# First MLP of a fused cross-attention and mixture-of-experts kernel: both first-layer products in three parts of high and low numbers, one bias added a stage earlier, VectorE's work per block in another order

## The chip, the cores and the metric

The kernel runs on one core of a Trainium2 chip. The metric is the device time of one execution in microseconds (us); for the kernel before, the median of three runs is shown beside the lowest and the highest.

## The reference

The input is x, 64 x 64 tokens of 128 numbers, a context of 64 x 64 x 96 and the weights. Four layers are added to x in turn, each of the normalised x:

```
x = x + xattn0(layernorm(x), ctx)   # attention with the 32 largest scores, a convolution along time, an MLP
x = x + ffn0(layernorm(x))          # router, 8 experts, two a token, limited capacity
x = x + xattn1(layernorm(x), ctx)
x = x + ffn1(layernorm(x))          # 8 experts with low-rank parts
```

The part that the change touches is the end of xattn0 and the router of ffn0:

```
xt = x_text + y                                     # y: the convolution
h  = layernorm(xt, g_ffn, b_ffn)
h  = gelu(h @ W1 + b1) @ W2 + b2                    # 128 -> 512 -> 128
xt = xt + h
xattn0 = layernorm(xt, g_norm_out, b_norm_out)      # g_norm_out: "gout", b_norm_out: "bout"
...
x  = x + xattn0
n  = layernorm(x)
logits = relu(n @ rw1 + rb1) @ rw2 + rb2            # 128 -> 512 -> 8, two largest of 8
```

## The kernel before

The 4096 tokens are 32 tiles of 128 rows, and all of x lies in SBUF (`G.X`, and `G.XT` for the branch). The program is a row of stages, each a block with one program an engine, written by hand with semaphores: set-up, first attention, `convolution` (L1005 on), `first_mlp_and_router` (L1088 on), first experts, combination with the second attention, second experts, combination. The order of each engine's instructions is the order in which they are written; no scheduler changes it.

`first_mlp_and_router` works in 8 blocks of 4 tiles, 512 tokens each. Each engine has a loop over steps t, in which several blocks are at different points:

- VectorE (`block_statistics`, L189; `normalise_block`, L208): statistics of XT for the MLP's norm (block t+2, first root), normalised rows `mlp_xs`; the addition of the second product to XT (block t-1, L1374) and its statistics (second root); the output norm into `mlp_nb`, times gout (L1386), added to x (L1387), and statistics of x (third root); the normalised x of block t-2 into XT (`xn`), which the router reads and SyncE writes out.
- GpSimd computes the inverse roots (L203, L205), one after each statistics, and adds two biases a block (`add_biases`): b2 to XT (L1217) and bout to X (L1218). From the third call on it waits until VectorE has normalised `mlp_nb` (semaphore `gained`), as the biases stand behind the second root in its order.
- TensorE transposes the normalised rows (L1240), makes the hidden product, four fp32 matmuls of 128x512 (L1247, two instructions each in the trace), the second product (L1276, 16 of 128x128), and for the router: transposes (L1269), the first product (L1292, again four of 128x512), the logits in four column groups (L1262), and their sums over the groups (L1285).
- ScalarE takes the transposes out of PSUM (L1317 with the norm's gain and bias, L1339 for the router), the gelu (L1323), the relu (L1342) and the logits (L1335).

One step of TensorE, in order: transposes of block t+1, hidden product of t, logits of t-3, router transposes of t-2, second product of t, sums of t-3, first router product of t-2. Behind the loop VectorE picks the two largest logits: a batch of the first 28 tiles (from L1062 in the trace), then one of the last four.

The convolution stage runs 8 steps of 16 channels. TensorE's small products (L1035) feed VectorE's scaling (L1045) and shift (L1051), GpSimd adds the result to XT (L1025), and SyncE loads the MLP's weights (semaphore `weights`, 8 loads).

The second experts of the program already multiply in three parts: a number is split into a high part, rounded to the type F32R by ScalarE (L2417), and a low part, the rest (VectorE, L2446); L2403 to L2405 are high x high, low x high and high x low.

Of the kernel before, what the change touches and what calls it, by code (L numbers as in the profile page):

```python
# [6 lines left out]
F32 = mybir.dt.float32  # L7
# [8 lines left out]
P = 128  # L16
# [3 lines left out]
TB = 4  # L20
# [972 lines left out]
def convolution(nc, C, A, G):  # L993
# [4 lines left out]
    with ExitStack() as ctx:  # L998
# [4 lines left out]
        with nc.Block() as block:  # L1003
# [36 lines left out]
            def _(dve):  # L1040
                for g in range(NG + 1):
# [5 lines left out]
                    if g > 0:  # L1047
# [4 lines left out]
                                          ALU.add).then_inc(s["y_shift"], 1)  # L1052

# [34 lines left out]
def first_mlp_and_router(nc, C, A, G):  # L1088
# [9 lines left out]
    with ExitStack() as ctx:  # L1098
        def two(name, shape):
            return [C.sb(f"{name}{j}", shape, ctx=ctx) for j in range(2)]  # L1100

        w1, rw1, w2, rw2, b2, gout, bout, rb2 = (G.mlp[n] for n in ("w1", "rw1", "w2", "rw2", "b2", "gout", "bout", "rb2"))
# [31 lines left out]
            "xs", "turned", "xf", "y", "y_taken", "biased", "gained", "xn", "turned1", "xf1", "logits", "logits_sb", "summed", "lg", "pick",  # L1134
# [28 lines left out]
        with nc.Block() as block:  # L1163
# [27 lines left out]
            def _(pool):  # L1191
# [22 lines left out]
                def add_biases(b):  # L1214
                    rows = slice(b * TB, (b + 1) * TB)
                    pool.wait_ge(s["xs"], b + 1)
                    pool.tensor_tensor(G.XT[:, rows, :], G.XT[:, rows, :], wide(b2[:].unsqueeze(1), [P, TB, D]), ALU.add)  # L1217
                    pool.tensor_tensor(G.X[:, rows, :], G.X[:, rows, :], wide(bout[:].unsqueeze(1), [P, TB, D]), ALU.add).then_inc(s["biased"], 1)  # L1218

                for t in range(-2, NBLK + 1):  # L1220
# [5 lines left out]
                    root_of(1, t - 1)  # L1226
                    if blk(t + 1):
                        if blk(t - 1):
                            pool.wait_ge(s["gained"], t)
                        add_biases(t + 1)  # L1230
# [3 lines left out]
            def _(pe):  # L1234
# [7 lines left out]

                def hidden(b):
                    pe.wait_ge(s["xf"], b + 1)
                    for c in range(NH):
                        after(pe, r_sb[c], b - 2)
                        pe.matmul(psh[c][:], w1[:, c * P:(c + 1) * P], xf[b % 2][:], start=True, stop=True).then_inc(h_ps[c], 1)  # L1247

                for t in range(-1, NBLK + 3):
# [37 lines left out]
                    if blk(t - 2):  # L1287
                        b = t - 2
                        pe.wait_ge(s["xf1"], b + 1)
                        for c in range(NH):  # L1290
                            after(pe, h_sb[c], min(t + 1, NBLK))
                            pe.matmul(psh[c][:], rw1[:, c * P:(c + 1) * P], xf1[b % 2][:], start=True, stop=True).then_inc(r_ps[c], 1)  # L1292
# [20 lines left out]
            def _(act):  # L1313
                act.preload_act_table(ACT.Gelu)
                def keep_turned(b):
                    act.wait_ge(s["turned"], b + 1)
                    act.activation(xf[b % 2][:], pst[:], ACT.Identity, scale=G.vec[:, gv:gv + 1],  # L1317
                                   bias=G.vec[:, bv:bv + 1]).then_inc(s["xf"], 1)

# [5 lines left out]
                for t in range(-1, NBLK + 3):  # L1325
                    if t == 0:
                        gelu(0)
                    if blk(t + 1):
                        keep_turned(t + 1)
                    if blk(t) and t > 0:  # L1330
                        gelu(t)
                    if blk(t - 3):
# [1286 lines left out]
```

## Time and profile before

| what | us |
|---|---|
| median of three runs | 935.64 |
| lowest, highest | 929.67, 935.94 |
| the profiled execution | 933.83 |
| its span, first to last instruction | 932.5 |
| TensorE busy in the span | 705.8 (76%) |
| VectorE busy | 672.9 (72%) |
| GpSimd busy | 571.7 (61%) |
| ScalarE busy | 472.9 (51%) |
| mean granted TensorE clock | 0.809 |

Each share is a mean over stages with different limits. The stage of the change lies between about 295 and 447 us. In the timeline an instruction stands with its start and its duration in us, and consecutive instructions of one line are one row with their count ("x4"); the brackets behind it give how long the engine was idle before it and which instruction ended that wait.

### The profile page before, as it was taken

The numbers are of one execution on the slowest core, as the hardware profiler recorded it, in microseconds if no ns is written. First come the engines' busy times: TensorE is split into PE (matmuls) and PEld (weight loads), VectorE is DVE, ScalarE is ACT, GpSimd is POOL, SyncE is SP. The second block draws the span as 40 slices with busy tenths as digits, with TensorE's granted clock in tenths as the row PEclk, the third lists the DMA queues.
The fourth block names the chain that finished last, engine by engine and source line by source line (L and its number), as shares of the span: only waits on it lengthen the run. The fifth ranks groups of instructions, "written<-read, shape, count | busy, mean of one in ns | idle before, by whom it ended". The sixth has DMA issues, their size and how long they took to land. (4 is left out here: it accounts for less than half of the span.)

```text
span 932.5 us, 20545 instructions
## 1 busy us (share of the span) xinstructions
PE 705.8 (76%) x6072; PEld 506.3 (54%) x6072; DVE 672.9 (72%) x3212; ACT 472.9 (51%) x1318; POOL 571.7 (61%) x931
## 2 busy tenths in 40 slices
PE   0687798958685999972498528998998875799960
PEld 0354455535375656631275416766665552699960
DVE  6898988879814788669111167588899986699964
ACT  3557655745400455440133165677777761577740
POOL 7698867666734765310677667345778867277770
PEclk9758777878755999996599855798889985899985
DMA  6300112699410978820366240000000003799818
GB/s 143 57 25 10 41 43 57 83 83 88 67 44 33 326 253 261 251 83 0 39 115 132 79 148 1 2 3 14 25 25 26 26 30 87 211 280 262 261 63 270
DMA packets 98828, 94.40 MB, mean 101 GB/s; under 512 B 37511, under 2 KB 82302, under 8 KB 98142
## 3 DMA queue, kind: packets, MB, share of 16 engines
q1 hardware_dynamic: 91268, 79.34, 34.1%
q0 software_dynamic: 6592, 13.58, 5.9%
q8 instruction: 50, 0.82, 0.4%
q14 instruction: 60, 0.49, 0.2%
q10 hardware_dynamic: 858, 0.17, 0.1%
HBM read 47.76 MB, written 43.19 MB: 98 GB/s over the span
## 5 line engine op out<-in xcount | busy, mean ns | idle before, releaser
L2436 POOL DMA_INDIRECT expert_pairs<-e_ys,e_home x78 | 75.4, 967 | 38.6 <-issue 23.5
L1776 POOL TENSOR_SCALAR a_kb<-a_kr,a_m,a_bk 128x128 f32<-128x128 f32 x128 | 57.9, 453 | 43.7 <-ACT a_kr L2015 31.5
L1794 POOL DMA_INDIRECT expert_slots<-r_rows,r_slotu x64 | 63.3, 989 | 27.9 <-issue 13.5
L950 DVE MATCH_REPLACE8 work<-m,work 128x64 f32<-128x64 f32 x384 | 75.6, 206 | 0.0
L1518 POOL DMA_INDIRECT ex_rows<-rows,slot_source x32 | 30.7, 960 | 53.3 <-POOLq L1163 43.8
L937 DVE MAX8 m<-work 128x8 f32<-128x64 f32 x384 | 57.0, 209 | 0.0
L1849 PE MATMUL a_pss<-a_kb,a_qt 32*64 32x256 f32 x512 | 42.3, 455 | 12.9 <-ACT a_pp L2000 10.9
L825 PE MATMUL psf<-filmw,us 97*128 97x512 f32 x64 | 48.7, 855 | 1.1 <-ACT FO L846 1.0
L2403 PE MATMUL e_ps<-e_XH,e_wh 128*128 128x256 f32 x156 | 48.1, 308 | 1.3 <-DVE e_XL L2448 1.3
L2202 DVE TENSOR_REDUCE a_mx<-a_pss 128x8 f32<-128x512 f32 x64 | 43.8, 684 | 7.1 <-PE a_pss L1849 6.8
L1570 ACT ACTIVATE ex_hs<-ex_psh,vec 128x512 f32<-128x512 f32 x32 | 22.0, 687 | 51.2 <-PE ex_psh L1551 50.5
L2405 PE MATMUL e_ps<-e_XH,e_wl 128*128 128x256 f32 x156 | 44.6, 286 | 0.0
L2404 PE MATMUL e_ps<-e_XL,e_wh 128*128 128x256 f32 x156 | 44.6, 286 | 0.0
L1995 ACT ACTIVATE a_pp<-a_dd 128x512 f32<-128x512 f32 x32 | 20.2, 631 | 43.0 <-DVE a_dd L2211 43.0
L1342 ACT ACTIVATE rt_rs<-mlp_psh,vec 128x512 f32<-128x512 f32 x32 | 22.0, 687 | 34.5 <-PE mlp_psh L1292 34.5
L1924 PE MATMUL a_psp<-ident,a_pp 128*128 128x128 f32 x256 | 38.1, 298 | 1.8 <-ACT a_pt L2048 1.8
L2253 DVE RECIPROCAL a_rt<-a_pso 128x128 f32<-128x128 f32 x31 | 29.5, 950 | 12.9 <-PE a_pso L1916 9.9
L1528 POOL DMA_INDIRECT planes<-ex_ys,slot_home x32 | 31.2, 976 | 11.4 <-issue 9.4
L808 PE MATMUL pss<-kb,qt 128*64 128x256 f32 x128 | 27.9, 525 | 13.4 <-ACT kb L846 13.3
L741 POOL TENSOR_TENSOR sc<-dd,pen 128x256 f32<-128x256 f32 x32 | 23.2, 725 | 22.6 <-ACT dd L846 22.6
L2211 DVE TENSOR_TENSOR a_dd<-a_mx,a_pss 128x512 f32<-128x512 f32 x64 | 35.4, 554 | 2.2
L2048 ACT ACTIVATE a_pt<-a_psp 128x512 f32<-128x512 f32 x64 | 35.5, 611 | 2.1 <-PE a_psp L1924 2.0
(464 smaller groups left out, 2404.1 us busy)
## 6 DMA issues: line engine op xcount, KB each, us to landing
expert_slots<-rt_unfilled SPq DMA_DIRECT2D x151, 130.0 KB, 3.0
ahead<-folded_weights SPq DMA_DIRECT2D x20, 386.0 KB
e_wf<-folded_weights SPq DMA_DIRECT2D x19, 386.0 KB, 3.9
planes<-rt_zeros SPq DMA_DIRECT2D x4, 1024.0 KB
ew<-in_L_ffn_ew SPq DMA_DIRECT2D x16, 256.0 KB, 3.8
pair_y<-expert_pairs SPq DMA_DIRECT2D x16, 256.0 KB, 6.0
e_xr<-expert_slots SPq DMA_DIRECT2D x27, 130.0 KB, 3.2
folded_weights<-fold_done SPq DMA_DIRECT2D x8, 384.0 KB, 4.1
```

Source lines behind the costliest of these rows:

```text
L825: pe.matmul(psf[:], us[j][:], G.filmw[:], start=True, stop=True).then_inc(s["film"], 1)
L937: mx = dve.max(m8[x.j][:, h, r, :], src[:, h, :])
L950: return own.did(dve.match_replace(wk_[x.j][:, h, :], m8[x.j][:, h, r, :], src[:, h, :], TAKEN))
L1776: m = pool.tensor_scalar(kb[a.j][:, :, h, :], k, m4[:, h:h + 1], bk4[:, h:h + 1], ALU.mult, ALU.add)
L1794: pool.indirect_dma_start(G.slots, bass.IndirectOffsetOnAxis(ap=slot[:, b, k, t:t + 1], axis=0), rb[b % NB][:, k, t, :], None).then_inc(se ...
L1849: mm = pe.matmul(pss[half][T * b:T * b + T, h, 0:HG * T], qt[g.j][rows, T * b:T * b + T], kb[g.j][rows, b, :, :], start=True, stop=True)
L1924: mm = pe.transpose(psp[half][:, k, :], pp[x.j][:, h:h + 2, :].rearrange("p h k -> p (h k)"), G.ident[:])
L2202: dve.tensor_reduce(m, scores(half), AX.X, ALU.min).then_inc(s["lowest"], 1)
L2403: pe.matmul(psh[m][c][:], wh[j][:, m, c, :], XH[j][:], start=True, stop=False)
L2404: pe.matmul(psh[m][c][:], wh[j][:, m, c, :], XL[j][:], start=False, stop=False)
L2405: pe.matmul(psh[m][c][:], wl[j][:, m, c, :], XH[j][:], start=False, stop=True).then_inc(h_ps[m][c], 1)
L2436: pool.indirect_dma_start(G.pair, bass.IndirectOffsetOnAxis(ap=home[i % NY][:, k:k + 1], axis=0), ys[i % NY][:, k, :], None).then_inc(kept ...
```

## The change

Both first-layer products (hidden L1247 and router L1292 of before) become three matmuls of type F32R each, high weights by high input, high by low and low by high (`product`). ScalarE rounds the weights' high parts at the stage's start and VectorE forms their low parts (in the steps t = -2 and -1). For each block ScalarE rounds the high part of the transposed input (`high_part`, and behind the router's copy), and GpSimd subtracts it from the whole (`low_part`), in its order behind the second root and ahead of the bias. TensorE waits for these low parts. In ScalarE's order the router's copy and its rounding now stand ahead of the copy of the logits.

The output norm's bias leaves GpSimd: VectorE adds it to x in the convolution stage, in four instructions of eight tiles each, in the steps 3 to 6, after a wait for all weight loads. In VectorE's loop the statistics of block t+2 move ahead of the normalisation of block t-2, and the normalisation, gain and addition of the output norm become eight scalar_tensor_tensor of one tile. GpSimd's wait for `gained` goes.

```diff
--- before.py
+++ after.py
@@ -1050,6 +1050,11 @@
+                    if g == 3:
+                        dve.wait_ge(s["weights"], 16 * 8)
+                    if 3 <= g < 7:
+                        rows = G.X[:, (g - 3) * NT // 4:(g - 2) * NT // 4, :]
+                        dve.tensor_tensor(rows, rows, wide(G.mlp["bout"][:].unsqueeze(1), [P, NT // 4, D]), ALU.add)
...
@@ -1214,19 +1221,23 @@
-                    pool.tensor_tensor(G.X[:, rows, :], G.X[:, rows, :], wide(bout[:].unsqueeze(1), [P, TB, D]), ALU.add).then_inc(s["biased"], 1)
...
+                def low_part(b, whole, parts, high, low):
+                    if blk(b):
+                        pool.wait_ge(high, b + 1)
+                        pool.tensor_tensor(parts[b % 2][:, 1, :], whole[b % 2][:], parts[b % 2][:, 0, :].bitcast(F32), ALU.subtract).then_inc(low, 1)
...
                     root_of(1, t - 1)
+                    low_part(t - 2, xf1, xf1s, s["x1_high"], s["x1_low"])
+                    low_part(t + 1, xf, xfs, s["x_high"], s["x_low"])
                     if blk(t + 1):
-                        if blk(t - 1):
-                            pool.wait_ge(s["gained"], t)
                         add_biases(t + 1)
                     root_of(2, t - 1)
@@ -1240,11 +1251,18 @@
+                def product(c, w, x):
+                    part = w[:, :, c * P:(c + 1) * P]
+                    pe.matmul(psh[c][:], part[:, 0, :], x[:, 0, :], start=True, stop=False)
+                    pe.matmul(psh[c][:], part[:, 0, :], x[:, 1, :], start=False, stop=False)
+                    return pe.matmul(psh[c][:], part[:, 1, :], x[:, 0, :], start=False, stop=True)
+
                 def hidden(b):
-                    pe.wait_ge(s["xf"], b + 1)
+                    pe.wait_ge(s["x_low"], b + 1)
+                    pe.wait_ge(s["w_low"], 1)
                     for c in range(NH):
                         after(pe, r_sb[c], b - 2)
-                        pe.matmul(psh[c][:], w1[:, c * P:(c + 1) * P], xf[b % 2][:], start=True, stop=True).then_inc(h_ps[c], 1)
+                        product(c, w1s, xfs[b % 2]).then_inc(h_ps[c], 1)
...
@@ -1286,10 +1304,11 @@
-                        pe.wait_ge(s["xf1"], b + 1)
+                        pe.wait_ge(s["x1_low"], b + 1)
+                        pe.wait_ge(s["w_low"], 2)
                         for c in range(NH):
                             after(pe, h_sb[c], min(t + 1, NBLK))
-                            pe.matmul(psh[c][:], rw1[:, c * P:(c + 1) * P], xf1[b % 2][:], start=True, stop=True).then_inc(r_ps[c], 1)
+                            product(c, rw1s, xf1s[b % 2]).then_inc(r_ps[c], 1)
@@ -1312,10 +1331,17 @@
+                act.activation(w1s[:, 0, :], w1[:], ACT.Copy).then_inc(s["w_high"], 1)
+                act.activation(rw1s[:, 0, :], rw1[:], ACT.Copy).then_inc(s["w_high"], 1)
...
+                def high_part(b):
+                    act.wait_ge(s["xf"], b + 1)
+                    act.activation(xfs[b % 2][:, 0, :], xf[b % 2][:], ACT.Copy).then_inc(s["x_high"], 1)
@@ -1327,16 +1353,24 @@
+                    if t == -1:
+                        high_part(0)
                     if blk(t) and t > 0:
                         gelu(t)
+                    if blk(t - 2):
+                        b = t - 2
+                        act.wait_ge(s["turned1"], b + 1)
+                        act.activation(xf1[b % 2][:], pst[:], ACT.Copy).then_inc(s["xf1"], 1)
+                        act.wait_ge(s["xf1"], b + 1)
+                        act.activation(xf1s[b % 2][:, 0, :], xf1[b % 2][:], ACT.Copy).then_inc(s["x1_high"], 1)
                     if blk(t - 3):
...
                         act.activation(lgt[:, b * TB:(b + 1) * TB, :].rearrange("p k t -> p (k t)"), psg[:], ACT.Copy).then_inc(s["logits_sb"], 1)
+                    if blk(t + 1) and t >= 0:
+                        high_part(t + 1)
                     if blk(t - 2):
                         b = t - 2
-                        act.wait_ge(s["turned1"], b + 1)
-                        act.activation(xf1[b % 2][:], pst[:], ACT.Identity).then_inc(s["xf1"], 1)
@@ -1358,15 +1392,18 @@
+                    if blk(t + 2):
+                        b = t + 2
+                        after(dve, s["xs"], b)
+                        block_statistics(dve, step, G.XT[:, b * TB:(b + 1) * TB, :], st[0]).then_inc(var[0], 1)
+                    if t in (-2, -1):
+                        whole, parts = ((w1, w1s), (rw1, rw1s))[t + 2]
+                        dve.wait_ge(s["w_high"], t + 3)
+                        dve.tensor_tensor(parts[:, 1, :], whole[:], parts[:, 0, :].bitcast(F32), ALU.subtract).then_inc(s["w_low"], 1)
                     if blk(last):
...
                         normalise_block(dve, xt, x, st[2]).then_inc(s["xn"], 1)
-                    if blk(t + 2):
-                        b = t + 2
-                        x = G.XT[:, b * TB:(b + 1) * TB, :]
-                        after(dve, s["xs"], b)
-                        block_statistics(dve, step, x, st[0]).then_inc(var[0], 1)
@@ -1377,14 +1414,16 @@
                         dve.wait_ge(root[1], close + 1)
-                        normalise_block(dve, nb, xt, st[1]).then_inc(s["gained"], 1)
-                        dve.wait_ge(s["gained"], close + 1)
-                        step.then(dve.tensor_tensor(nb[:], nb[:], wide(gout[:].unsqueeze(1), [P, TB, D]), ALU.mult))
-                        step.then(dve.tensor_tensor(x, x, nb[:], ALU.add))
+                        for k in range(TB):
+                            m = dve.scalar_tensor_tensor(nb[:, k, :], xt[:, k, :], st[1]["mv"][:, k, 0:1], gout[:], ALU.subtract, ALU.mult)
+                        step.then(m)
+                        for k in range(TB):
+                            m = dve.scalar_tensor_tensor(x[:, k, :], nb[:, k, :], st[1]["rstd"][:, k:k + 1], x[:, k, :], ALU.mult, ALU.add)
+                        step.then(m)
```

VectorE's order in a step in the middle, before, from the addition of the second product on (`mlp_ln0`, `1`, `2` are the three norms' statistics, `mlp_psy` the second product, `rt_lg` the logits):

```order
L1374 TENSOR_TENSOR XT<-XT,mlp_psy0 128x512
L192 BN_STATS mlp_ln1_st<-XT 128x6 x4
L195 BN_AGGR mlp_ln1_mv<-mlp_ln1_st 128x2 x4
L211 TENSOR_SCALAR mlp_xs1<-XT,mlp_ln0_mv,mlp_ln0_rstd 128x128 x4
L211 TENSOR_SCALAR mlp_nb<-XT,mlp_ln1_mv,mlp_ln1_rstd 128x128 x4
L1386 TENSOR_TENSOR mlp_nb<-mlp_nb,mlp_gout 128x512
L1387 TENSOR_TENSOR X<-X,mlp_nb 128x4x128
L192 BN_STATS mlp_ln2_st<-X 128x6 x4
L195 BN_AGGR mlp_ln2_mv<-mlp_ln2_st 128x2 x4
L1355 TENSOR_TENSOR rt_lg<-rt_psg,mlp_rb2 128x32
L211 TENSOR_SCALAR XT<-X,mlp_ln2_mv,mlp_ln2_rstd 128x128 x4
L192 BN_STATS mlp_ln0_st<-XT 128x6 x4
```

The same step now:

```order
L1411 TENSOR_TENSOR XT<-XT,mlp_psy0 128x512
L192 BN_STATS mlp_ln1_st<-XT 128x6 x4
L195 BN_AGGR mlp_ln1_mv<-mlp_ln1_st 128x2 x4
L211 TENSOR_SCALAR mlp_xs1<-XT,mlp_ln0_mv,mlp_ln0_rstd 128x128 x4
L1422 SCALAR_TENSOR_TENSOR mlp_nb<-XT,mlp_ln1_mv,mlp_gout 128x128 x4
L1425 SCALAR_TENSOR_TENSOR X<-mlp_nb,mlp_ln1_rstd,X 128x128 x4
L192 BN_STATS mlp_ln2_st<-X 128x6 x4
L195 BN_AGGR mlp_ln2_mv<-mlp_ln2_st 128x2 x4
L1389 TENSOR_TENSOR rt_lg<-rt_psg,mlp_rb2 128x32
L192 BN_STATS mlp_ln0_st<-XT 128x6 x4
L195 BN_AGGR mlp_ln0_mv<-mlp_ln0_st 128x2 x4
L211 TENSOR_SCALAR XT<-X,mlp_ln2_mv,mlp_ln2_rstd 128x128 x4
```

The three rows from `mlp_nb` to X became two of four scalar_tensor_tensor, and the statistics of the coming block (`mlp_ln0_st`) stand ahead of the normalisation with the third root, not behind it.

GpSimd's order in such a step before, from the second root to the third:

```order
L203 TENSOR_SCALAR mlp_ln1_v<-mlp_ln1_mv 128x4
L205 TENSOR_TENSOR mlp_ln1_rstd<-mlp_ln1_v,minus_half 128x4
L1217 TENSOR_TENSOR XT<-XT,mlp_b2 128x512
L1218 TENSOR_TENSOR X<-X,mlp_bout 128x4x128
L203 TENSOR_SCALAR mlp_ln2_v<-mlp_ln2_mv 128x4
L205 TENSOR_TENSOR mlp_ln2_rstd<-mlp_ln2_v,minus_half 128x4
```

And now (`rt_xf` and `mlp_xf` are the router's and the MLP's transposed input, `rt_xfs` and `mlp_xfs` their two parts):

```order
L203 TENSOR_SCALAR mlp_ln1_v<-mlp_ln1_mv 128x4
L205 TENSOR_TENSOR mlp_ln1_rstd<-mlp_ln1_v,minus_half 128x4
L1229 TENSOR_TENSOR rt_xfs1<-rt_xf1,rt_xfs1 128x512
L1229 TENSOR_TENSOR mlp_xfs0<-mlp_xf0,mlp_xfs0 128x512
L1224 TENSOR_TENSOR XT<-XT,mlp_b2 128x512
L203 TENSOR_SCALAR mlp_ln2_v<-mlp_ln2_mv 128x4
L205 TENSOR_TENSOR mlp_ln2_rstd<-mlp_ln2_v,minus_half 128x4
```

Two subtractions stand where one bias addition left, so three instructions of 128x512 lie between the two roots instead of two.

## Rows read from the trace of the kernel before

**Rows 1.** Busy time by stretches; us, busy us of each engine, PEclk, DMA share, GB/s

```profile
302.00:308.00 6.00, 5.27 (x8) 2.31 (x9) 4.29 (x13) 2.36 (x4) 3.80 (x5) 0.59 1.01 423
308.00:345.00 37.00, 37.00 (x215) 25.88 (x214) 29.88 (x118) 18.93 (x29) 25.46 (x33) 1.00 0.89 275
399.00:407.00 8.00, 7.01 (x38) 3.20 (x31) 5.07 (x23) 4.05 (x7) 1.27 (x2) 1.00 0.27 104
```

**Rows 2.** Timeline of TensorE, first hidden product of two blocks; columns: start us, us, engine, line, operation, out<-in

```profile
358.27 3.60 PE L1247 MATMUL mlp_psh<-mlp_xf,mlp_w 128*128 128x512 f32 x8
...
371.63 0.59 PE L1247 MATMUL mlp_psh<-mlp_xf,mlp_w 128*128 128x512 f32 x1
```

**Rows 3.** Timeline of VectorE and GpSimd, one round, from block 3's addition on

```profile
348.57 0.65 DVE L1374 TENSOR_TENSOR XT<-XT,mlp_psy 128x512 f32<-128x512 f32 x1
...
352.02 1.11 DVE L211 TENSOR_SCALAR mlp_nb<-XT,mlp_ln_mv,mlp_ln_rstd 128x128 f32<-128x128 f32 x4 [0.47 <-POOL mlp_ln_rstd L205]
353.17 0.69 DVE L1386 TENSOR_TENSOR mlp_nb<-mlp_nb,mlp_gout 128x512 f32<-128x512 f32 x1
353.21 1.77 POOL L1217 TENSOR_TENSOR XT<-XT,mlp_b 128x512 f32<-128x512 f32 x1 [1.23 <-DVE mlp_nb L211]
...
353.89 1.64 DVE L1387 TENSOR_TENSOR X<-X,mlp_nb 128x512 f32<-128x512 f32 x1
...
354.94 1.72 POOL L1218 TENSOR_TENSOR X<-X,mlp_bout 128x512 f32<-128x512 f32 x1
...
355.56 0.87 DVE L192 BATCH_NORM_STATS2 mlp_ln_st<-X 128x6 f32<-128x128 f32 x4
...
357.25 1.04 POOL L205 TENSOR_TENSOR mlp_ln_rstd<-mlp_ln_v,minus_half 128x4 f32<-128x4 f32 x1
...
358.32 1.12 DVE L211 TENSOR_SCALAR XT<-X,mlp_ln_mv,mlp_ln_rstd 128x128 f32<-128x128 f32 x4 [1.40 <-POOL mlp_ln_rstd L205]
...
359.35 0.86 DVE L192 BATCH_NORM_STATS2 mlp_ln_st<-XT 128x6 f32<-128x128 f32 x4
...
360.55 0.66 DVE L1374 TENSOR_TENSOR XT<-XT,mlp_psy 128x512 f32<-128x512 f32 x1
```

**Rows 4.** Line L1374: min/median/max ns, first and last start

```profile
L1374 DVE TENSOR_TENSOR XT<-XT,mlp_psy x8: 652/668/689, 312.6 to 395.3; 128x512 f32<-128x512 f32 x8
```

**Rows 5.** Timeline of the second experts, their three-part products

```profile
836.00 0.28 PE L2403 MATMUL e_ps<-e_XH,e_wh 128*128 128x256 f32 x1
...
836.59 0.28 PE L2405 MATMUL e_ps<-e_XH,e_wl 128*128 128x256 f32 x1
...
836.97 0.63 ACT L2417 ACTIVATE e_wh<-e_wf 128x512 fp32r<-128x512 f32 x1
```

**Rows 6.** VectorE's scalar_tensor_tensor: two lines, min/median/max ns, first and last start

```profile
L555 DVE SCALAR_TENSOR_TENSOR toe<-toe x1: 296/296/296, 12.8 to 12.8; 128x128 f32<-128x128 f32 x1
...
L958 DVE SCALAR_TENSOR_TENSOR pr<-work,ee x32: 424/426/796, 40.4 to 251.9; 128x256 f32<-128x256 f32 x32
```

**Rows 7.** Timeline of the stage's start

```profile
302.73 5.78 PE L1247 MATMUL mlp_psh<-mlp_xf,mlp_w 128*128 128x512 f32 x8 [0.87 <-ACT mlp_xf L1317]
303.43 1.26 POOL L1217 TENSOR_TENSOR XT<-XT,mlp_b 128x512 f32<-128x512 f32 x1
303.49 3.02 DVE L211 TENSOR_SCALAR mlp_xs<-XT,mlp_ln_mv,mlp_ln_rstd 128x128 f32<-128x128 f32 x4 [1.48 <-POOL mlp_ln_rstd L205]
```

**Rows 8.** Timeline of the stage's end, VectorE and ScalarE

```profile
394.13 0.19 DVE L1355 TENSOR_TENSOR rt_lg<-rt_psg,mlp_rb 128x32 f32<-128x32 f32 x1 [4.43 <-PE rt_psg L1285]
...
404.09 1.11 DVE L211 TENSOR_SCALAR XT<-X,mlp_ln_mv,mlp_ln_rstd 128x128 f32<-128x128 f32 x4 [1.40 <-POOL mlp_ln_rstd L205]
...
407.43 0.60 ACT L1339 ACTIVATE rt_xf<-mlp_pst 128x512 f32<-128x512 f32 x1
...
408.83 0.39 DVE L1062 TENSOR_REDUCE rt_m<-rt_lg 128x28 f32<-128x224 f32 x1
```

**Rows 9.** Timeline of the convolution, VectorE

```profile
273.49 0.69 DVE L1045 TENSOR_TENSOR ym<-psy,FO 128x512 f32<-128x512 f32 x1 [2.13 <-PE psy L1035]
```

More of the change, by code:

```diff
@@ L1100, in two @@
             return [C.sb(f"{name}{j}", shape, ctx=ctx) for j in range(2)]
-        w1, rw1, w2, rw2, b2, gout, bout, rb2 = (G.mlp[n] for n in ("w1", "rw1", "w2", "rw2", "b2", "gout", "bout", "rb2"))
+        w1, rw1, w2, rw2, b2, gout, rb2 = (G.mlp[n] for n in ("w1", "rw1", "w2", "rw2", "b2", "gout", "rb2"))
+        w1s, rw1s = (C.sb(n, [D, 2, HID], F32R, ctx) for n in ("mlp_w1s", "rt_w1s"))
+        xfs, xf1s = ([C.sb(f"{n}{j}", [D, 2, TB * P], F32R, ctx) for j in range(2)] for n in ("mlp_xfs", "rt_xfs"))
         pick = C.sb("rt_pick", [P, 32], ctx=ctx)
@@ L1133, in first_mlp_and_router @@
         s = {n: C.sem("mlp_" + n) for n in (
-            "xs", "turned", "xf", "y", "y_taken", "biased", "gained", "xn", "turned1", "xf1", "logits", "logits_sb", "summed", "lg", "pick",
+            "w_high", "w_low", "xs", "turned", "xf", "x_high", "x_low", "y", "y_taken", "biased", "xn", "turned1", "xf1", "x1_high", "x1_low", "logits", "logits_sb", "summed", "lg", "pick",
             "d", "exp", "sel", "pos", "dve", "pool", "counts", "zeros", "cleared", "rows",
@@ L1216, in add_biases @@
                     pool.wait_ge(s["xs"], b + 1)
-                    pool.tensor_tensor(G.XT[:, rows, :], G.XT[:, rows, :], wide(b2[:].unsqueeze(1), [P, TB, D]), ALU.add)
-                    pool.tensor_tensor(G.X[:, rows, :], G.X[:, rows, :], wide(bout[:].unsqueeze(1), [P, TB, D]), ALU.add).then_inc(s["biased"], 1)
-                for t in range(-2, NBLK + 1):
+                    pool.tensor_tensor(G.XT[:, rows, :], G.XT[:, rows, :], wide(b2[:].unsqueeze(1), [P, TB, D]), ALU.add).then_inc(s["biased"], 1)
+                def low_part(b, whole, parts, high, low):
+                    if blk(b):
+                        pool.wait_ge(high, b + 1)
+                        pool.tensor_tensor(parts[b % 2][:, 1, :], whole[b % 2][:], parts[b % 2][:, 0, :].bitcast(F32), ALU.subtract).then_inc(low, 1)
+                for t in range(-2, NBLK + 2):
                     root_of(0, t + 2)
@@ L1379, in _ @@
                         after(dve, s["turned"], b - 1)
-                        normalise_block(dve, xs[b % 2], x, st[0]).then_inc(s["xs"], 1)
+                        normalise_block(dve, xs[b % 2], G.XT[:, b * TB:(b + 1) * TB, :], st[0]).then_inc(s["xs"], 1)
                     if blk(close):
```

## Prediction

> **What bounds the kernel now.** I read the busy table by stretches first, then the timeline of TensorE alone, then that of VectorE with GpSimd, and last the two ends of the stage. The stretch of blocks 0 to 2 shows TensorE busy 37.00 of 37.00 us at full clock, with VectorE at 29.88 [rows 1]: in the steady part TensorE bounds the stage. Its round is the distance of two first hidden products, 358.27 and 371.63: 13.36 us. The row of eight instructions lasts 3.60 and a single one 0.59, so the instructions start (3.60 − 0.59) / 7 = 0.43 apart, and one fp32 product of 512 columns, which is two of them, costs 0.86 [rows 2].
>
> VectorE's round is the distance of two additions of the second product, 348.57 and 360.55: 11.98 us [rows 3]. It runs ahead of TensorE and pays at the end, where it waits 4.43 us for TensorE at 394.13 [rows 8]. The eight additions stretch from 312.6 to 395.3 [rows 4], 82.7 us. So what a faster TensorE is worth is limited at once by VectorE's 11.98: seven rounds of it are 83.9, hardly another length. The question is therefore what the change does to VectorE's round, not to TensorE's.
>
> **The change, part by part.**
> TensorE. The second experts already run such products: six of 256 columns start between 836.00 and 836.59, 0.118 apart [rows 5]. With 512 columns I take twice that, 0.236, so three are 0.71 in place of 0.86: 0.15 less a product, eight products a round, 1.2 less: 12.2. The bounds of one 512-column instruction are 0.215 (half the 0.43 of an fp32 one, if fp32 is two such passes) and 0.43 (no gain at all).
>
> VectorE, what goes. From 352.02 to 355.56, 3.54 us, stand the normalisation, the gain and the addition to x [rows 3]. Eight scalar_tensor_tensor of 128 columns replace them. The one such row takes 0.296 [rows 6]; in four statistics of 128 columns, 0.87 together [rows 3], one follows the other by about 0.2. I take two groups of 0.87 with hand-overs, 1.9; the bounds are 1.7 (half of 0.424, the row of 256 columns, eight times) and 2.3 (eight of 0.296 end to end, or two groups as the 1.11 of four normalisations). The statistics of the coming block, 359.35 to 360.55, 1.20 us, move into the wait of 1.40 for the third root at 358.32 [rows 3]; that wait covers them. VectorE's round is then 11.98 − 3.54 − 1.20 + 1.90 = 9.14 if nobody disturbs it.
>
> VectorE, what comes. GpSimd disturbs it. Before, GpSimd's two bias additions began when the normalisation was done (a wait of 1.23 at 353.21), and while they ran VectorE's addition at 353.89 took 1.64, against 0.69 for the same shape just before [rows 3]: 0.95 lost. At the start the normalisations at 303.49 took 3.02 in place of 1.11 under the two additions of 303.43 [rows 7, 3]: 1.91 for two, again 0.95 each. The statistics at 355.56 took their 0.87 beside such an addition [rows 3], so they aren't held. A scalar_tensor_tensor is: one of 256 columns took 796 ns at most where the median is 426 [rows 6]. Now GpSimd issues three additions or subtractions (low part of the router's input, low part of the next block's input, b2) right behind the second root, and VectorE's eight instructions wait for that same root. So three times one VectorE instruction loses between 0.95 and the whole 1.26 of an undisturbed GpSimd addition [rows 7]: 2.85 to 3.8, I take 3.2. VectorE's round becomes 9.14 + 3.2 = 12.3. That is over TensorE's 12.2: the bound moves to VectorE, at almost the round that it had.
>
> The Trainium skill, page "SBUF — State Buffer", section "SBUF: two separate sides", says that VectorE and GpSimd share a port pair as an exclusive lock, that a VectorE instruction with two SBUF inputs takes part in it, and that whoever starts second blocks fully. The 1.64 against 0.69 agrees with it; by that rule rival A below can't happen, and it speaks against the change. The skill's page "VectorE: DVE Perf Modes", section "TRN2 errata — SBUF-src ops pay a fixed extra latency per instruction", gives (N+151)/0.96 ns, an estimate of 0.29 for 128 columns: eight end to end are 2.3 and the round is 0.4 longer; the 0.87 for four statistics is against counting them end to end.
>
> The chain of additions, 82.7 before. First interval: no router part yet, two GpSimd instructions, 9.14 + 2.1 = 11.3. Five rounds of 12.3 are 61.5. Last interval: only the router part, 10.3. Together 83.1: +0.4. From the last addition to the last normalised block (395.3 to 404.09 [rows 4, 8]) the shorter update saves 0.7 and one held instruction with its hand-over costs 1.2: +0.5.
>
> From there to the routing's first batch, 404.09 to 408.83, 4.74 us [rows 8]: ScalarE now copies the block's transpose (0.60 at 407.43) and rounds it (0.63 [rows 5]) ahead of the copy of the logits, on which the sums and the batch hang. Transposed at 1.9 behind the normalisation's start, copied 2.5, rounded 3.1, logits 3.8, sums and their addition 5.0: +0.3. The last block's own logits lie beside the batch's work on VectorE.
>
> The start. The first hidden product waits for the high part (0.63 on ScalarE) and the low part (1.26 on GpSimd), with hand-overs about 2.0 later than 302.73 [rows 7]. It then runs at the low clock, of which this stretch shows 0.59 granted [rows 1]: 12 instructions of 0.43 are 5.2, where the eight take 5.78 now. And GpSimd no longer adds the second bias there. Between +0.2 and +1.3; I take +0.8.
>
> Costs put at nothing. The weights' high parts, two of 0.63 on ScalarE, and low parts, two of 0.69 as the row of 353.17 [rows 3], fall into VectorE's waits of 1.48 for the first roots [rows 7]; without cover they'd cost 1.4. Output norm's bias in the convolution: four additions of twice 512 columns, 1.38 each, in a stage where VectorE waits 2.13 a step for TensorE [rows 9]; if each is held by GpSimd's sum of that step it is 2.6, and four lag by some 0.5 each, 2 in all, of which the step without addition gives most back. GpSimd's eight additions that go (354.94 [rows 3]) bring nothing by themselves; GpSimd isn't the bound.
>
> Sum: +0.4 + 0.5 + 0.3 + 0.8 = +2.0 us on the profiled execution's 933.83 (its span is 932.5): 935.8. The median of the three runs is 935.64, 1.8 above the profiled one, so the forecast is no change that can be told: a measurement of this kernel tells apart about 1%, 9.3 us.
>
> **The rivals.**
> A: VectorE's new instructions aren't held, because by the time they start GpSimd still waits for ScalarE's high parts. Then VectorE's round is 9.1 and TensorE's 12.2 sets the pace: 48 products between the first and the last addition, 0.15 each, −7.2; start +0.8; and the last two router products wait for 0.63 + 1.26, of which about 0.5 lies beside the sums, +2.8. That is 930.2, and 927.3 with products of 0.645. For it: ScalarE is busy about half the time [rows 1], and its queue could be late. Against it: the high parts stand before the relus in ScalarE's order, some microseconds ahead of the second root.
> B, the other side: GpSimd's subtraction with the rounded output takes 1.78, as its addition did when it alternated with VectorE (1.77 and 1.72 [rows 3]), not 1.26. Two a round are +1.0, six rounds +6.2, start and tail 0.5 each: +7.2, 943.0. It decides from about 1.78 on: there the total is 9.2 and crosses 1%. For it: GpSimd and VectorE alternate instruction by instruction in the same rows. Against it: what I already charge VectorE covers part of that.
> C, the change doesn't do what it says: 512 columns cost 0.43 in this type too. A product is 1.29, the 48 of them +20.6, with start and tail 958. The 0.118 of 256 columns speaks against it [rows 5].
> D: with VectorE as the bound TensorE pauses in each round, and the granted clock falls, as it stands at 0.59 in the first six microseconds [rows 1]. It would bite at the end, where router product, logits, transposes and sums (about 6 us) stand on the path: +6, 942. Against it: 399 to 407 has TensorE busy 7.01 of 8 at full clock [rows 1].
>
> **How the numbers follow.** Forecast 0.62, with a range of its own of 932 to 942 (a group of eight at 1.7 to 2.3 and a loss of 2.85 to 3.8 are −0.55 to +1.0 a round, over six rounds −3 to +6; the low side needs TensorE's products under 0.71 as well). A 0.12, B 0.16, C 0.03, D 0.07. The range from 927 (A at its lower bound) to 944 (B, D) leaves out C and the ends of the others. Faster by over 1% needs A and a start without its delay: 0.04. Slower by over 1%: half of B, C and some of D: 0.14. The rest, 0.82, is within 1%.
>
> **What would show it.** In the changed kernel's profile: three products spaced 0.236; VectorE's additions of the second product about 12.3 apart; among the eight scalar_tensor_tensor three that last about 1.2 while GpSimd's subtractions run beside them; TensorE with pauses in each round, where it had none. Additions 11 or less apart would make the sum too high (A), subtractions well over 1.3 too low (B). An end of the convolution more than 1 us later would refute the cover of the bias.

## The result and the profile after

Over 20 runs each, the changed kernel's median is 936.78 us and that of before 932.86, 3.9 apart. The ratio on record, which counts fast runs alone, is 1.0075 with a 95% interval of 1.0051 to 1.0099; why it is larger than the quotient of the medians, 1.0042, isn't shown. The kernel is slower by less than 1%, as was forecast, but by some 7 us (4.8 to 9.2) where the sum said 2.0.

The eight additions of the second product, line L1411 now ([rows 4]; min/median/max ns, first and last start):

```profile
L1411 DVE TENSOR_TENSOR XT<-XT,mlp_psy x8: 681/683/689, 316.4 to 402.1; 128x512 f32<-128x512 f32 x8
```

They stretch over 85.6 us where they took 82.7. The parts of the stage, from VectorE's rows of both profiled executions (the first two rows are the stage's start and end before, the third its end now; its start now, 298.32, is shown further down):

```profile
295.39 0.87 DVE L192 BATCH_NORM_STATS2 mlp_ln_st<-XT 128x6 f32<-128x128 f32 x4 [2.95 <-PEq L1003]
...
446.45 0.17 DVE L1461 CAST slot_home<-rt_home 128x32 uint32<-128x32 f32 x1
```

```profile
453.71 0.17 DVE L1500 CAST slot_home<-rt_home 128x32 uint32<-128x32 f32 x1
```

| part, us | before | forecast | after |
|---|---|---|---|
| first statistics to first addition | 17.17 | +0.8 | 18.10 (+0.93) |
| first to last addition | 82.70 | +0.4 | 85.64 (+2.94) |
| to the last normalisation | 8.83 | +0.5 | 9.57 (+0.74) |
| to the routing's first batch | 4.74 | +0.3 | 5.27 (+0.53) |
| to the slot tables, the end | 37.62 | 0 | 36.81 (−0.81) |
| stage | 151.06 | +2.0 | 155.39 (+4.33) |

One round of VectorE and GpSimd in the timeline, from block 4's addition to the next; it answers to [rows 3]:

```profile
366.07 0.68 DVE L1411 TENSOR_TENSOR XT<-XT,mlp_psy 128x512 f32<-128x512 f32 x1
...
368.47 1.04 POOL L205 TENSOR_TENSOR mlp_ln_rstd<-mlp_ln_v,minus_half 128x4 f32<-128x4 f32 x1
...
369.48 1.27 POOL L1229 TENSOR_TENSOR rt_xfs<-rt_xf,rt_xfs 128x512 fp32r<-128x512 f32 x1
369.55 4.22 DVE L1422 SCALAR_TENSOR_TENSOR mlp_nb<-XT,mlp_ln_mv,mlp_gout 128x128 f32<-128x128 f32 x4 [0.47 <-POOL mlp_ln_rstd L205]
...
370.71 1.33 POOL L1229 TENSOR_TENSOR mlp_xfs<-mlp_xf,mlp_xfs 128x512 fp32r<-128x512 f32 x1
...
372.00 1.35 POOL L1224 TENSOR_TENSOR XT<-XT,mlp_b 128x512 f32<-128x512 f32 x1
...
373.80 1.14 DVE L1425 SCALAR_TENSOR_TENSOR X<-mlp_nb,mlp_ln_rstd,X 128x128 f32<-128x128 f32 x4
...
376.66 1.04 POOL L205 TENSOR_TENSOR mlp_ln_rstd<-mlp_ln_v,minus_half 128x4 f32<-128x4 f32 x1
...
377.73 1.12 DVE L211 TENSOR_SCALAR XT<-X,mlp_ln_mv,mlp_ln_rstd 128x128 f32<-128x128 f32 x4 [1.40 <-POOL mlp_ln_rstd L205]
378.76 0.69 DVE L1411 TENSOR_TENSOR XT<-XT,mlp_psy 128x512 f32<-128x512 f32 x1
```

378.76 − 366.07 is a round of 12.69. At 369.48 and 369.55 GpSimd's first subtraction and VectorE's update start together, both released by the second root. The first four scalar_tensor_tensor take 4.22, the second four, after GpSimd is through, 1.14. So three of them wait for one GpSimd instruction each, 3.08 in all. Of all 32 of the first kind (L1422) the median is one that waited ("held"), the shortest is one that didn't:

```profile
L1422 DVE SCALAR_TENSOR_TENSOR mlp_nb<-XT,mlp_ln_mv,mlp_gout x32: 337/1349/1385, 320.0 to 407.3; 128x128 f32<-128x128 f32 x32
```

TensorE, in the same round and by stretches (columns as in [rows 1]):

```profile
366.21 0.66 PE L1287 MATMUL mlp_pst<-ident,XT 128*128 128x128 f32 x4 [0.58 <-DVE XT L211]
...
371.09 0.48 PE L1256 MATMUL mlp_psh<-rt_xfs,rt_w1s 128*128 128x512 f32 x1
...
373.94 0.60 PE L1251 MATMUL mlp_pst<-ident,mlp_xs 128*128 128x128 f32 x4
```

```profile
302.00:308.00 6.00, 1.12 (x4) 0.72 (x4) 4.68 (x13) 1.41 (x2) 4.36 (x5) 0.50 0.63 262
308.00:345.00 37.00, 33.91 (x222) 29.26 (x222) 31.58 (x120) 21.35 (x33) 23.71 (x33) 0.96 0.86 285
399.00:407.00 8.00, 3.47 (x24) 1.84 (x23) 5.03 (x21) 2.91 (x5) 3.76 (x5) 0.96 0.64 243
407.00:414.00 7.00, 5.88 (x24) 3.62 (x24) 4.65 (x24) 2.96 (x5) 1.26 (x2) 0.80 0.06 21
```

Twelve instructions fill 371.09 to 373.94: 0.237 apart, 0.71 a product. TensorE now pauses, 33.91 busy of 37 where it was 37.00; at 366.21 it waits for VectorE's normalisation. So VectorE is now the bound, as the experiments below confirm.

### The profile page after: what moved, and what is told of

Its sections match the earlier page's. It is cut to its first block and busy times, and to the rows that moved or that the text cites. A ratio compares the mean times of both kernels' runs of the same rounds, so it can differ in the third digit from the quotient of the medians.

```text
span 939.2 us, 20723 instructions
## 1 busy us (share of the span) xinstructions
PE 706.0 (75%) x6136; PEld 525.9 (56%) x6136; DVE 690.2 (73%) x3234; ACT 482.3 (51%) x1336; POOL 579.3 (62%) x939
## 5 line engine op out<-in xcount | busy, mean ns | idle before, releaser
L825 PE MATMUL psf<-filmw,us 97*128 97x512 f32 x64 | 50.7, 887 | 2.9 <-ACT FO L846 2.9
L958 DVE SCALAR_TENSOR_TENSOR pr<-work,ee 128x256 f32<-128x256 f32 x32 | 15.5, 485 | 29.8 <-ACT ee L895 26.9
```

Of the source, the lines that this page charges most:

```text
L825: pe.matmul(psf[:], us[j][:], G.filmw[:], start=True, stop=True).then_inc(s["film"], 1)
```

## The experiments

Theory H is that of the forecast: each GpSimd instruction of 128x512 that runs beside VectorE's update holds one of its instructions, and this sets the round. Rival R: TensorE's wait for the low parts, which come through a copy, a rounding and a subtraction, sets it. Each run is read by the line of its eight additions: the three profiles in which nothing that bears on this stretch (by H) was changed have 85.59, 85.64 and 85.65 us, while single times of the kernel before differ by 1.4% (927.01 to 940.01). All but one of the kernels below were run once, so their times as a whole decide nothing.

**b2 ahead of the second root.**

```diff
+                    if blk(t + 1):
+                        add_biases(t + 1)
                     root_of(1, t - 1)
...
-                    if blk(t + 1):
-                        add_biases(t + 1)
                     root_of(2, t - 1)
```

> GpSimd adds b2 ahead of the second root instead of behind the two low parts; nothing else moves. Theory H (each GpSimd instruction of 128x512 that runs beside VectorE's eight scalar_tensor_tensor costs VectorE's round about 1.03, 3.08 for the three of now): only two are left there, the round goes from 12.69 to 11.66, and the eight additions of the second product stretch over 79.5 us instead of 85.6. Rival R (TensorE's wait for the low parts sets the round, through copy, high part and low part): the low parts come no earlier, the eight additions stay at 85.6 or more.

```profile
L1411 DVE TENSOR_TENSOR XT<-XT,mlp_psy x8: 674/680/689, 315.7 to 396.0; 128x512 f32<-128x512 f32 x8
```

80.4: four of the rounds are 11.65 or 11.66, H's number; one is 12.62, in which b2 met the normalisation with the third root. R's 85.6 isn't there. The sum is 0.9 over the expected 79.5 by that one round. At the start the low part of the first block stood behind b2 here, and the first addition came 19.83 behind the first statistics.

**One more GpSimd addition, behind and ahead.** The same line at two places:

```diff
+                    if blk(t + 1) and t >= 1:
+                        step.then(pool.tensor_tensor(spend[:], wide(gout[:].unsqueeze(1), [P, TB, D]), wide(b2[:].unsqueeze(1), [P, TB, D]), ALU.add))
```

> One more GpSimd addition of 128x512 into a tile that nobody reads, behind the bias addition and ahead of the third root, in six of the steps. Theory H: one more of VectorE's scalar_tensor_tensor is held in each of six rounds, 6 x 1.03 = +6.2 on the eight additions (91.8). Rival R: it stands behind both low parts, so they come when they came, +0. A third, Q (GpSimd's own time sets the round): +1.27 a round, 7.6.

> The same additional GpSimd addition, but ahead of the second root, where VectorE adds the second product and takes statistics. Theory H: nothing of two SBUF inputs runs on VectorE there, so 0 to +0.3 a round (85.6 to 87.4). Q: GpSimd is 1.27 longer in each round, +7.6. R: the low parts come behind it, up to 1.27 later where GpSimd has no pause ahead of the root, 0 where it has.

Behind the low parts, then ahead of the second root:

```profile
L1414 DVE TENSOR_TENSOR XT<-XT,mlp_psy x8: 678/682/687, 313.6 to 405.9; 128x512 f32<-128x512 f32 x8
```

```profile
L1414 DVE TENSOR_TENSOR XT<-XT,mlp_psy x8: 676/682/689, 311.3 to 400.0; 128x512 f32<-128x512 f32 x8
```

92.3 and 88.7. Behind, the round is 13.8, 1.1 more: nearer to H's 1.03 than to Q's 1.27, and not R's 0. Ahead, 88.7 is over the 85.6 to 87.4 that H had: three rounds grow by 0.19 to 0.25, as expected, since the second root comes 0.2 later (VectorE waits 0.68 for it instead of 0.47). Two grow by 1.15 and 1.17, which H had not foreseen: there the added instruction started beside a normalisation, of four tensor_scalar, which took 1.99 and 2.05 in place of 1.1. So tensor_scalar, which reads one tile, is held too. (The sixth round, +0.07, holds none of the six added instructions; the fifth holds two.) In one of the three the added instruction runs beside VectorE's statistics, and these keep their 0.87:

```profile
350.12 1.28 POOL L1239 TENSOR_TENSOR rt_spend<-mlp_gout,mlp_b 128x512 f32<-128x512 f32 x1
...
350.60 0.87 DVE L192 BATCH_NORM_STATS2 mlp_ln_st<-XT 128x6 f32<-128x128 f32 x4
```

The same work on the same engine costs about 1.1 or 0.2, by what VectorE does meanwhile. Q, GpSimd's own time, falls: it would cost 1.27 in every round.

**High parts alone on TensorE.**

```diff
-                    pe.matmul(psh[c][:], part[:, 0, :], x[:, 0, :], start=True, stop=False)
-                    pe.matmul(psh[c][:], part[:, 0, :], x[:, 1, :], start=False, stop=False)
-                    return pe.matmul(psh[c][:], part[:, 1, :], x[:, 0, :], start=False, stop=True)
+                    return pe.matmul(psh[c][:], part[:, 0, :], x[:, 0, :], start=True, stop=True)
...
-                    pe.wait_ge(s["x_low"], b + 1)
+                    pe.wait_ge(s["x_high"], b + 1)
```

> TensorE leaves out the two products with low parts and waits for the high parts alone; GpSimd still makes the low parts, which nobody reads. The output is that of the high parts alone. TensorE's round has 8 x 0.475 = 3.8 us less work and its products wait 1.27 less. Theory H: VectorE sets the round, the eight additions stay at 85.6 (84.5 to 86.5). R: the round loses at least the low part's 1.27, the eight additions fall to 77 or less.

```profile
L1409 DVE TENSOR_TENSOR XT<-XT,mlp_psy x8: 679/681/689, 311.8 to 397.4; 128x512 f32<-128x512 f32 x8
```

85.6, the same, with two thirds of the products gone and no wait for low parts. R falls: neither TensorE's products nor its wait for low parts set this stretch.

**Two GpSimd instructions ahead of the root.**

```diff
+                    low_part(t + 1, xf, xfs, s["x_high"], s["x_low"])
+                    if blk(t + 1):
+                        add_biases(t + 1)
                     root_of(1, t - 1)
                     low_part(t - 2, xf1, xf1s, s["x1_high"], s["x1_low"])
```

> GpSimd makes the low part of the next block's MLP input and adds b2 ahead of the second root; only the router's low part stays behind it. ScalarE rounds that input right behind its copy. Theory H: one scalar_tensor_tensor is held a round (1.03), and two instructions of 1.27 stand ahead of the root in a stretch of 1.94 without instructions of two SBUF inputs, so the root comes up to 0.6 later: VectorE's round is 9.61 + 1.03 + 0.6 = 11.2 at most, under TensorE's 12.2. The eight additions stretch over 76 to 79 us (TensorE's: 82.7 less 48 products x 0.145 = 75.7). Rival R: the router's low part comes as before, 84 or more.

```profile
L1408 DVE TENSOR_TENSOR XT<-XT,mlp_psy x8: 675/679/689, 303.5 to 384.1; 128x512 f32<-128x512 f32 x8
```

80.5, and 76 to 79 was expected: a miss, though R's 84 isn't there. The second and third round are VectorE's at 11.25, as said; two of the later ones are TensorE's at 12.03, which is busy 35.00 of the 35 us from 345 to 380. The expectation had charged TensorE's saving to the whole stretch, while TensorE gets it only where it is the bound; that this is all of the miss wasn't tested.

**The old update, and low parts on VectorE.**

```diff
-                            m = dve.scalar_tensor_tensor(nb[:, k, :], xt[:, k, :], st[1]["mv"][:, k, 0:1], gout[:], ALU.subtract, ALU.mult)
...
+                        step.then(normalise_block(dve, nb, xt, st[1]))
+                        step.then(dve.tensor_tensor(nb[:], nb[:], wide(gout[:].unsqueeze(1), [P, TB, D]), ALU.mult))
+                        step.then(dve.tensor_tensor(x, x, nb[:], ALU.add))
```

> The eight scalar_tensor_tensor become again four tensor_scalar and two tensor_tensor of 128x512, at the same place; all else as in the changed kernel. Theory H: three GpSimd instructions hold three of the tensor_scalar just as they hold three scalar_tensor_tensor (3.08), and the six take 1.11 + 0.69 + 0.69 and hand-overs, 2.6 in place of 2.4: +0.2 a round, the eight additions at 87. Rival S (it is the form of the new instructions, slow or held more, that costs): the round falls back towards 12.0, the additions to 84 or less.

The other kernel has `low_part` on VectorE, ahead of its wait for the second root, and none on GpSimd:

```diff
+                    low_part(t - 2, xf1, xf1s, s["x1_high"], s["x1_low"])
+                    low_part(t + 1, xf, xfs, s["x_high"], s["x_low"])
                     if blk(close):
                         x = G.X[:, close * TB:(close + 1) * TB, :]
                         dve.wait_ge(root[1], close + 1)
```

> VectorE makes both low parts itself, behind the normalisation for the coming block, and GpSimd none. VectorE gets 2 x 0.69 more work in a round that it bounds. Theory H: two held instructions go (2 x 1.03), the wait of 0.47 for the second root is filled, so the round is 12.69 - 2.06 - 0.47 + 1.3 = 11.5 and the additions 79 to 82. Without a lock (VectorE's work alone counts): +1.3 a round, 94.

```profile
L1411 DVE TENSOR_TENSOR XT<-XT,mlp_psy x8: 677/680/687, 306.2 to 392.8; 128x512 f32<-128x512 f32 x8
```

```profile
L1409 DVE TENSOR_TENSOR XT<-XT,mlp_psy x8: 680/682/689, 308.6 to 387.6; 128x512 f32<-128x512 f32 x8
```

86.6: the form of the update is worth 0.1 a round, so S falls; the four tensor_scalar of the update take 4.02 to 4.04 here in place of 1.11. 79.1: giving the engine that bounds two more instructions makes its round shorter, from 12.69 to 11.3 (11.9 in two of the last rounds, where VectorE waits for ScalarE's high parts). The two start 0.6 apart and last 0.69 each, where on GpSimd each cost VectorE 1.03, and they fill the 0.47 that VectorE had waited for the second root.

**The rest of the change with fp32 products.** The products, their waits and all high and low parts are as before the change.

> The rest of the change alone: fp32 products as before, no high and low parts; bias in the convolution, VectorE's new order and instructions, GpSimd with b2 alone. Theory H: VectorE's round would be 9.61 + 1.03 = 10.6, but TensorE's 13.36 is back as the bound: the additions stretch over 81.5 to 83 (before: 82.7), and of the shorter update only some 0.7 at the stage's end is left; the time is that of before within 2 us. Rival R says the same of TensorE. If the new order alone cost anything, the additions would take over 83.

```profile
L1392 DVE TENSOR_TENSOR XT<-XT,mlp_psy x8: 678/680/686, 314.4 to 397.1; 128x512 f32<-128x512 f32 x8
```

82.7, that of before. The first three rounds are 10.6, VectorE's as said (9.61 and one held instruction), the later ones up to 13.36, TensorE's: it bounds, and in this stretch the new order neither gains nor costs.

At the stage's end it does cost in this profile, against the expectation: the batch begins 8.79 behind the last normalisation, where before took 4.74, and the whole stage takes 155.08, about what the changed kernel took (the single times, 939.03 and 938.41 for the kernel before, tell nothing). The router's product of the second last block shows one part, here and then before:

```profile
404.13 5.38 PE L1253 MATMUL mlp_psh<-rt_xf,mlp_rw 128*128 128x512 f32 x8
```

```profile
401.19 3.68 PE L1292 MATMUL mlp_psh<-rt_xf,mlp_rw 128*128 128x512 f32 x8
```

The granted clock was 0.63 from 404 to 408, where before had 1.00. The other part is ScalarE's order: in two blocks TensorE's sums start 2.8 behind its logits, where before took 1.8, because the copy of the transposes stands ahead of that of the logits.

**Putting it together, and ScalarE's order at the end.** The first kernel takes the low parts on VectorE and b2 ahead of the root, and:

```diff
+                        if b == 0:
+                            pe.matmul(psh[c][:], w1[:, c * P:(c + 1) * P], xf[0][:], start=True, stop=True).then_inc(h_ps[c], 1)
...
+                                pe.matmul(psh[c][:], rw1[:, c * P:(c + 1) * P], xf1[b % 2][:], start=True, stop=True).then_inc(r_ps[c], 1)
...
+                    if t == NBLK + 1:
+                        keep_logits(t - 3)
```

> Both low parts on VectorE as before in the run with low parts on VectorE, b2 ahead of the second root, the first block's hidden product and the last block's router product in fp32 (nobody waits for parts there), and at the end the logits of the second last block leave PSUM ahead of the last block's transposes. Theory H: no GpSimd instruction of 128x512 runs beside VectorE's update any more, its round is 11.27 - 1.03 = 10.3, TensorE's 12.0 to 12.2 bounds: the eight additions stretch over 76 to 78 us, the first stands 17.2 behind the stage's start as before, the first batch 4.7 to 5.0 behind the last normalisation: the stage is about 6 us shorter than before, 0.4 to 0.8% of the whole. If rather the three-part products themselves cost (R), no order of GpSimd's brings the stage under that of before.

The second is the changed kernel with the last two lines of that diff alone.

> The changed kernel, with the copy of the logits of the second last block ahead of the copy and the rounding of the last block's transposes on ScalarE. From the last normalisation to the first batch the changed kernel takes 5.27, before 4.74. If ScalarE's order makes the difference, 4.0 to 4.7 at the full clock, and up to 1.5 more where TensorE's granted clock is low there; if not, 5.3 or more. All else stays: round 12.69, additions 85.6.

```profile
L1425 DVE TENSOR_TENSOR XT<-XT,mlp_psy x8: 655/680/684, 304.7 to 383.4; 128x512 f32<-128x512 f32 x8
```

```profile
346.77 0.60 PE L1244 MATMUL mlp_pst<-ident,mlp_xs 128*128 128x128 f32 x4
...
354.66 1.13 DVE L1439 SCALAR_TENSOR_TENSOR mlp_nb<-XT,mlp_ln_mv,mlp_gout 128x128 f32<-128x128 f32 x4
...
355.83 1.14 DVE L1442 SCALAR_TENSOR_TENSOR X<-mlp_nb,mlp_ln_rstd,X 128x128 f32<-128x128 f32 x4
...
358.79 0.60 PE L1244 MATMUL mlp_pst<-ident,mlp_xs 128*128 128x128 f32 x4
...
359.70 1.30 POOL L1224 TENSOR_TENSOR XT<-XT,mlp_b 128x512 f32<-128x512 f32 x1
359.76 2.09 DVE L211 TENSOR_SCALAR XT<-X,mlp_ln_mv,mlp_ln_rstd 128x128 f32<-128x128 f32 x4 [1.40 <-POOL mlp_ln_rstd L205]
```

```profile
345.00:360.00 15.00, 15.00 (x97) 12.28 (x96) 11.57 (x54) 11.15 (x18) 6.58 (x10) 1.00 0.73 244
```

The first kernel is a little faster than before: median 926.04 against 932.64 over 12 and 17 runs, ratio 0.9955 with an interval (0.9916 to 0.9993) that is barely clear of 1. Its profiled stage takes 146.65 where before took 151.06. VectorE's two groups now take 1.13 and 1.14, undisturbed, TensorE is busy without a pause, and its round is 12.02 (346.77 to 358.79). So R falls here too: with the three-part products the stage is shorter than before. It is 4.4 shorter and not the expected 6. The additions take 78.6, a little over the 76 to 78; at 359.70 b2 still meets a normalisation (2.09 where 1.12 is undisturbed). The first addition stands at 18.25 behind the first statistics, not 17.2, the first fp32 product having taken 6.70 for 5.78; the batch begins 4.26 behind the last normalisation, earlier than the 4.7 to 5.0. Several changes are in this one kernel, so what each is worth alone it doesn't show.

In the second, the batch begins 4.14 behind the last normalisation where it was 5.27, as expected of the order. But from there to the slot tables it takes 39.07 instead of 36.81: VectorE waits 1.13 for the last block's own logits and 0.91 for TensorE's positions, where it had waited 0.24 in all, and from 423 to 425 the granted clock is 0.50 where the changed kernel had 1.00. In this one profile the order alone brings nothing.

## Why the prediction came out as it did

**The mechanism was right.** The bound moved from TensorE to VectorE, by GpSimd's three instructions behind the second root: one instruction less there took 1.03 from the round, one more added 1.1, and taking two thirds of the products and a wait from TensorE changed nothing. The forecast's loss was 3.2 a round, measured 3.08. The Trainium skill, page "SBUF — State Buffer", section "SBUF: two separate sides", calls the port pair an exclusive lock and says the loser blocks fully: 1349 ns for a held instruction against 337 agrees, and so does the GpSimd addition that ran free beside statistics. The prediction named two SBUF inputs alone, while that section of the Trainium skill has a second condition beside it, a 2-port perf mode. The held tensor_scalar has one input tile, so if the rule covers it, it is by that second one, which no run here shows. The rule says nothing on when GpSimd starts, so it didn't exclude rival A, though the prediction said so; A fell by the rows: the subtraction at 369.48 starts with the second root.

**The size that was off** is the term "I take two groups of 0.87 with hand-overs, 1.9". The two groups take 1.14 each, 2.4 with hand-overs, over the upper bound of 2.3. So VectorE's undisturbed round is 12.69 − 3.08 = 9.61, not 9.14. The rounds came out 0.39 over the 12.3, five times, and the first and last interval 0.3 each: the 2.5 by which the chain of additions is above the sum. The nearer row was the four normalisations of [rows 3] at 1.11: they read two operands of one number a row, the new ones one such operand and two tiles, the statistics none. I had taken that row as the far bound and the statistics as the value; which operand makes the difference wasn't tested. By the Trainium skill's page "VectorE: DVE Perf Modes", section "TRN2 errata — SBUF-src ops pay a fixed extra latency per instruction", whose formula is for tensor_tensor, eight were estimated at 2.3 and the round 0.4 longer; I held the 0.87 against it. The measured sum, 2.28 without hand-overs, sides with that estimate, though its parts differ: a single one takes 337 ns at least, not 290, and they start 0.27 apart.

**TensorE's product** was 0.71 as forecast, and the subtraction with rounded output has medians of 1.27 and 1.33, not B's 1.78 (line L1229, min/median/max ns):

```profile
L1229 POOL TENSOR_TENSOR mlp_xfs<-mlp_xf,mlp_xfs x8: 1266/1334/1349, 306.7 to 383.4; 128x512 fp32r<-128x512 f32 x8
L1229 POOL TENSOR_TENSOR rt_xfs<-rt_xf,rt_xfs x8: 1261/1266/1269, 331.4 to 415.1; 128x512 fp32r<-128x512 f32 x8
```

**The convolution** cost nothing, by the cover that was named:

```profile
281.04 1.22 DVE L1057 TENSOR_TENSOR X<-X,mlp_bout 128x1024 f32<-128x1024 f32 x1
281.27 2.13 POOL L1025 TENSOR_TENSOR XT<-XT,yn 128x512 f32<-128x512 f32 x1 [2.15 <-DVE yn L1051]
283.25 0.69 DVE L1045 TENSOR_TENSOR ym<-psy,FO 128x512 f32<-128x512 f32 x1 [0.99 <-PE psy L1035]
```

The bias takes 1.22, TensorE's wait shrinks from 2.13 [rows 9] to 0.99, and GpSimd's sum beside it grows to 2.13. From the first scaling to the next stage's first statistics both kernels take 28.73.

**The start** was +0.93 for +0.8, and that it fits is luck. The parts are late by a little more than the 2.0 that was said, the first product starting 2.36 later than before:

```profile
298.32 0.87 DVE L192 BATCH_NORM_STATS2 mlp_ln_st<-XT 128x6 f32<-128x128 f32 x4 [2.94 <-PEq L1003]
...
306.70 1.27 POOL L1229 TENSOR_TENSOR mlp_xfs<-mlp_xf,mlp_xfs 128x512 fp32r<-128x512 f32 x1
...
308.02 0.79 PE L1256 MATMUL mlp_psh<-mlp_xfs,mlp_w1s 128*128 128x512 f32 x1 [3.23 <-POOL mlp_xfs L1229]
...
310.31 0.63 PE L1258 MATMUL mlp_psh<-mlp_xfs,mlp_w1s 128*128 128x512 f32 x1
...
311.04 0.40 PE L1257 MATMUL mlp_psh<-mlp_xfs,mlp_w1s 128*128 128x512 f32 x1
...
316.42 0.69 DVE L1411 TENSOR_TENSOR XT<-XT,mlp_psy 128x512 f32<-128x512 f32 x1 [1.31 <-PE mlp_psy L1294]
```

Of the first block's twelve instructions about six ran 0.43 apart, at the low clock, then 0.24. In the profiles of four kernels that start alike (additional addition behind and ahead, old update, ScalarE's order at the end) all did, and the first addition stood at 19.15, 19.52, 19.14 and 19.17 behind the first statistics, 1.0 to 1.4 later than here. The first of them:

```profile
304.12 0.79 PE L1259 MATMUL mlp_psh<-mlp_xfs,mlp_w1s 128*128 128x512 f32 x1 [3.23 <-POOL mlp_xfs L1230]
...
308.98 0.55 PE L1261 MATMUL mlp_psh<-mlp_xfs,mlp_w1s 128*128 128x512 f32 x1
```

The sum had all twelve at the low clock, and with that the start costs 2.0 to 2.4, over the upper bound of 1.3. It had 1.2 come back behind the later start; from the first product to the first addition it is 9.45 in this run where before took 9.83, so 0.4 come back.

**The end** went as said, 0.74 and 0.53 for 0.5 and 0.3:

```profile
411.63 1.12 DVE L211 TENSOR_SCALAR XT<-X,mlp_ln_mv,mlp_ln_rstd 128x128 f32<-128x128 f32 x4 [1.40 <-POOL mlp_ln_rstd L205]
...
414.41 0.63 ACT L1365 ACTIVATE rt_xfs<-rt_xf 128x512 fp32r<-128x512 f32 x1
414.95 0.58 ACT L1369 ACTIVATE XF<-rt_psg 128x512 f32<-128x512 f32 x1
...
416.90 0.39 DVE L1067 TENSOR_REDUCE rt_m<-rt_lg 128x28 f32<-128x224 f32 x1
```

At 414.41 the rounding stands ahead of the logits' copy at 414.95. Behind the batch's start 0.81 come back: VectorE waits 0.24 for TensorE's positions, before 1.08. Rival D came in small: the granted clock is 0.80 from 407 to 414, where before had 1.00, behind TensorE's pauses (3.47 busy of the eight us ahead). From the last normalisation to the batch the two kernels with the added GpSimd addition took 5.93 and 6.19, that with the old update 5.21.

So the profiled stage is 4.3 longer, near the distance of the medians (3.9) and a little under the interval of the ratio (4.8 to 9.2). Other executions of the same start and end can cost more: the kernels with the added addition and with the old update have that code, and less what their chain of additions grew over the changed kernel's (6.66, 3.05 and 0.96) their stages are 6.9, 7.5 and 5.5 longer than before's. How much of the measured ratio lies at the start and how much at the end isn't settled by single profiles, and before's own two ends are known from one. The rest of the two profiled executions' difference (940.5 less 933.83, 6.7) lies outside the stage, 2.9 of it ahead and 0.6 given back behind: the convolution's first scaling is at 269.59 instead of 266.66, in code that is the same, and in the experiments' profiles between 255.25 and 267.93. This says nothing on the change. In rival A's paragraph the lower bound adds up to 927.1 and not 927.3; nothing hangs on it.

## What to carry to other kernels

Before work is moved from a bounding TensorE to the side engines, count what each new GpSimd instruction will run beside: next to VectorE's scalar_tensor_tensor or tensor_scalar it cost VectorE 1.0 to 1.1 of its 1.27, next to statistics or an addition from PSUM 0.2 or less. Place such instructions by VectorE's order, or give them to VectorE itself where 0.69 there replaces a loss of 1.03. Several instructions of 128 columns are better sized by the row whose operands are nearest than by the fastest row of that width. And a term that depends on when the clock rises needs more than one profile.

## What was not expected

A four-instruction group of scalar_tensor_tensor with per-row operands takes 1.14 (337 to 347 ns each), against 0.87 for four statistics of the same width. And two more instructions on the engine that bounds made its round 1.4 us shorter (12.69 to 11.3), because they left GpSimd and filled a wait of VectorE's.
